# Queries written from PSUM into the heads' layout by two engines instead of six small DMAs, and a wait for output weights cut in two

## The reference, cut to what matters

```python
# layer 1, attention: latents = layernorm(x) [2, 512, 1024], H = 16 heads, KV = 4 groups of G = 4 heads, HD = 96
hidden = jnp.concatenate([context, latents], axis=1)            # 1536 rows
q = (latents @ Wq.T).reshape(b, q_len, H, HD)
k = (hidden @ Wk.T).reshape(b, s_len, KV, HD)
v = (hidden @ Wv.T).reshape(b, s_len, KV, HD)
scores = jnp.einsum('bkgqd,bksd->bkgqs', q, k) * scale
attn = jax.nn.softmax(scores, axis=-1)
out = jnp.einsum('bkgqs,bksd->bkgqd', attn, v)
return out.reshape(b, q_len, H * HD) @ Wo.T                     # added to x, times tanh(g_xattn[1])
# layer 1, feed-forward: router softmax, top 8 of 64 experts, mix of expert biases, added to x
```

## Time and profile before

| | us |
|---|---|
| median of 3 runs | 1075.05 (1074.87 to 1076.71) |
| profiled execution, its own time | 1076.0 |
| its span, first to last instruction | 1074.2 |
| PE busy | 1039.8 (97%) |
| DVE, ACT, POOL busy | 621.9, 620.1, 644.2 |
| units 0 to 127 start | 336.92 to 1026.02 |

### The profile page before, as it was taken

One profiled execution on the slowest core, in us unless ns is written; L12 is line 12 of the kernel. 1 busy time (PEld: TensorE's weight loads), 2 busy tenths in 40 slices (PEclk: granted clock), 3 DMA queues, 4 the chain that ended last, 5 costly groups with the idle time before them and its releaser, 6 DMA issues.

```text
span 1074.2 us, 18361 instructions
## 1 busy us (share of the span) xinstructions
PE 1039.8 (97%) x7242; PEld 587.5 (55%) x7242; DVE 621.9 (58%) x1068; ACT 620.1 (58%) x687; POOL 644.2 (60%) x348
## 2 busy tenths in 40 slices
PE   9999999999999989999999999999999999998895
PEld 4555434444544556566666666665665665555552
DVE  6889759654123555545545645655654655666666
ACT  5786435431223587665666765666765566577853
POOL 4476887242001588656668856658866667678751
PEclk9999999999999999999999999999999999999996
DMA  9886753842234999999999999999999999999993
GB/s 345 262 291 216 226 192 101 179 74 56 72 110 114 178 218 213 214 210 182 202 183 216 184 212 199 168 216 191 188 209 209 181 186 187 169 176 177 177 198 118
DMA packets 520265, 198.75 MB, mean 185 GB/s; under 512 B 485668, under 2 KB 500900, under 8 KB 520180
## 3 DMA queue, kind: packets, MB, share of 16 engines
q1 hardware_dynamic: 520180, 197.58, 88.3%
HBM read 56.88 MB, written 13.63 MB: 66 GB/s over the span
## 4 chain that ended last, share of the span: by engine, by line
PE 78%; POOL 9%; DMA 4%; DVE 3%; issue 3%; ACT 2%; SPq 1%; POOLq 0%; DVEq 0%; ACTq 0%
PE ps L566 27%; PE ps L806 21%; PE ps L780 12%; PE ps L821 10%; PE ps L823 5%; POOL p L1718 2%; POOL region_c L1718 2%; POOL region_y L1718 2%; DMA ln_t<-stage 1%; PE ps L588 1%; POOL x_res L1718 1%; DVE p_max L1553 1%; DMA region_o<-region_y 1%; PE ps L707 1%; DMA stage<-ctx_t_in 1%
## 5 line engine op out<-in xcount | busy, mean ns | idle before, releaser
L1718 POOL TENSOR_TENSOR region_y<-p,region_b 128x1536 f16<-128x1536 f32 x128 | 396.8, 3100 | 278.9 <-ACT region_b L1256 251.8
L1246 ACT ACTIVATE p<-ps,p_max 128x1536 f32<-128x1536 f32 x128 | 197.1, 1540 | 205.9 <-DVE p_max L1553 205.9
L1553 DVE TENSOR_REDUCE p_max<-ps 128x1 f32<-128x1536 f32 x128 | 225.0, 1757 | 131.3 <-PE ps L806 131.3
L806 PE MATMUL ps<-region_q,region_c 96*128 96x512 f16 x1152 | 269.9, 379 | 0.8 <-DMA region_c<-region_q 0.8
L821 PE MATMUL ps<-region_q,region_c 128*128 128x192 f16 x1536 | 207.6, 246 | 5.0 <-DVE logit L1578 3.4
L1256 ACT ACTIVATE region_b<-ps,p_max 128x1536 f16<-128x1536 f32 x128 | 196.4, 1534 | 25.9 <-DMA region_c<-region_b 25.6
L823 PE MATMUL ps<-region_q,region_o 128*128 128x96 f16 x1536 | 202.4, 206 | 0.0
L806 PEld LDWEIGHTS ps<-region_q,region_c 96*128 96x128 f16 x1152 | 105.3, 98 | 109.0 <-ACT region_b L1256 1.1
L821 PEld LDWEIGHTS ps<-region_q,region_c 128*128 128x128 f16 x1536 | 150.0, 98 | 21.7 <-DVE logit L1578 4.2
L823 PEld LDWEIGHTS ps<-region_q,region_o 128*128 128x128 f16 x1536 | 150.1, 98 | 13.9
L566 PE MATMUL ps<-region_w,region_q 128*128 128x512 f16 x576 | 136.1, 382 | 5.0 <-POOL region_w L1718 2.9
(11 more groups left out here) (149 smaller groups left out, 1105.7 us busy)
## 6 DMA issues: line engine op xcount, KB each, us to landing
stage<-ctx_in SPq DMA_DIRECT2D x16, 512.0 KB, 4.6
stage<-ctx_t_in SPq DMA_DIRECT2D x15, 512.0 KB, 8.7
stage<-wq_in SPq DMA_DIRECT2D x16, 384.0 KB, 4.0
stage<-wo_in SPq DMA_DIRECT2D x16, 384.0 KB, 4.3
k_scratch<-region_o SPq DMA_DIRECT2D x12, 384.0 KB, 6.5
region_q<-k_scratch SPq DMA_DIRECT2D x8, 576.0 KB, 5.6
region_q<-v_scratch SPq DMA_DIRECT2D x8, 576.0 KB, 6.1
x_res<-x_in SPq DMA_DIRECT2D x8, 512.0 KB, 8.7
```

The source lines that it names most:

```text
L806: ins = nc.tensor.matmul(bank(NSB * (m % 2) + sb_), q_head[0:HD, b, h, hq, qt * P:(qt + 1) * P], k_head[0:HD, b, hk, sb_ * 512:(sb_ + 1) * ...
L1246: nc.scalar.activation(p32[:, m % 2, :], rows, ACT.Exp, bias=p_max[:, m % 4:m % 4 + 1], accum_out=den[:, m % 4:m % 4 + 1]).then_inc(e32_ok, 1)
L1553: nc.vector.reduce_max(p_max[:, m % 4:m % 4 + 1], rows, axis=AX, negate=True).then_inc(max_ok, 1)
L1718: return nc.gpsimd.tensor_tensor(out, a, b, op)
```

## The change

Three parts.

1. On the host the columns of the query weights are put in another order within each group: block j gets the 96 columns of head j, and behind them columns 32j to 32j + 31 of head 3. So rows 0 to 95 of a product's block are head j, and rows 96 to 127 a third of head 3.
2. `take_q` and `take_low_q` write two pieces each, 96 partitions and 32 partitions, into `q_head` itself. `load_q`, `q_blk` and the semaphores `q_ld` are gone. `q_hi` and `q_free` count to two for a block; PE waits for `q_free` (six for a step) ahead of a step's first scores. From the third step on, ACT waits until the scores that read the old queries are done.
3. `out_product` with even w waits for the first two pieces of the output weights, with odd w for all four.

```diff
+        def q_rows(j):
+            own, last = slice(0, HD), slice(j * 32, (j + 1) * 32)
+            return ((j, own, own), (G - 1, last, slice(HD, P)))
...
-            def load_q(t, j):
-                sp.wait_ge(q_free, NJ * t + j + 1)
-                row = j * P
-                while row < (j + 1) * P:
-                    h, d = row // HD, row % HD
-                    n = min(HD - d, (j + 1) * P - row)
-                    sp.dma_start(q_head[d:d + n, t % B, h, :, :], q_blk[row - j * P:row - j * P + n, j, :, :]
-                                 ).then_inc(q_ld[t % B], 16)
-                    row += n
...
-                if q_end(m) is not None:
-                    if t > 0 and q_end(m) == 0:
-                        sp.wait_ge(sc_ready, UPS * t)
-                    load_q(t + 1, q_end(m))
...
-                    pe.wait_ge(q_ld[b], 6 * use(t, B))
+                    pe.wait_ge(q_free, 2 * NJ * (t + 1))
...
-                    pe.wait_ge(w_split, wo_n(w // 16) + RING)
+                    pe.wait_ge(w_split, wo_n(w // 16) + RING // 2 * (w % 2 + 1))
...
-                if t > 0:
-                    act.wait_ge(q_ld[(t - 1) % B], 6 * use(t - 1, B))
-                nc.scalar.activation(q_blk[:, j, HI, :], bank(at), ACT.Copy, scale=SCALE).then_inc(q_hi, 1)
+                if t >= B:
+                    act.wait_ge(sc_ready, UPS * (t - 1))
+                for h, rows, part in q_rows(j):
+                    nc.scalar.activation(q_head[rows, t % B, h, HI, :], bank(at)[part, :], ACT.Copy, scale=SCALE
+                                         ).then_inc(q_hi, 1)
...
-                dve.wait_ge(q_hi, n + 1)
-                nc.vector.scalar_tensor_tensor(q_blk[:, j, LO, :], bank(at), SCALE, q_blk[:, j, HI, :],
-                                               ALU.mult, ALU.subtract).then_inc(q_free, 1)
+                for k, (h, rows, part) in enumerate(q_rows(j)):
+                    dve.wait_ge(q_hi, 2 * n + k + 1)
+                    nc.vector.scalar_tensor_tensor(q_head[rows, t % B, h, LO, :], bank(at)[part, :], SCALE,
+                                                   q_head[rows, t % B, h, HI, :], ALU.mult, ALU.subtract
+                                                   ).then_inc(q_free, 1)
...
     wq = L1_xattn_Wq.T.reshape(NC, P, KV, QG).transpose(2, 1, 0, 3).reshape(KV * P, NC, QG)
+    order = np.concatenate([np.r_[j * HD:(j + 1) * HD, (G - 1) * HD + j * 32:(G - 1) * HD + (j + 1) * 32]
+                            for j in range(NJ)])
+    wq = wq[:, :, order]
```

More of the change, by code:

```diff
@@ L108, in flamingo @@
         v_head = view(region_q, 4 * SL, 2 * NS * VW).rearrange("p (b s w) -> p b s w", b=2, s=NS)
-        q_blk = view(region_q, 10752, NJ * 2 * QL).rearrange("p (j h s) -> p j h s", j=NJ, h=2)
         o_t = view(region_q, 13824, 2 * 2 * QG).rearrange("p (r h j q) -> p r h j q", r=2, h=2, j=NJ)
@@ L210, in flamingo @@
         v_ld = [sem(f"v_ld{b}") for b in range(B)]
-        q_ld = [sem(f"q_ld{b}") for b in range(B)]
         q_ready, q_hi, q_free = sem("q_ready"), sem("q_hi"), sem("q_free")
@@ L491, in _ @@
                 ring(s, stage[:, s, 0:c1 - c0], eb_d[:, c0:c1], w_split, W_WQ0 + s + 1)
-            for j in range(NJ):
-                load_q(0, j)
             sp.wait_ge(v_lo_ok, 5 * 4 + 2)
@@ L830, in _ @@
                 if j == 2:
-                    pe.wait_ge(q_free, 1)
+                    pe.wait_ge(q_free, 2)
                 q_product(6 + j % 2, 0, j, None)
@@ L861, in side_free @@
                     pe.wait_ge(v_lo_ok, 5 * 4 + 2 + sum(v in V_AT for v in before))
-                pe.wait_ge(q_free, NJ + sum(q_end(v) is not None for v in before))
+                pe.wait_ge(q_free, 2 * (NJ + sum(q_end(v) is not None for v in before)))
                 if any(wo_at(v) is not None for v in before):
@@ L1537, in take_low_q @@
             def take_low_q(n, at):
-                j = n % NJ
-                dve.wait_ge(q_hi, n + 1)
-                nc.vector.scalar_tensor_tensor(q_blk[:, j, LO, :], bank(at), SCALE, q_blk[:, j, HI, :],
-                                               ALU.mult, ALU.subtract).then_inc(q_free, 1)
+                t, j = n // NJ, n % NJ
+                for k, (h, rows, part) in enumerate(q_rows(j)):
[3 more added lines that the diff above has]
+                                                   ).then_inc(q_free, 1)
             def add_out(at, w):
```

## The result

Measured: 1069.57 us median (1068.31 to 1070.53, 6 runs) against 1075.89 (1074.87 to 1078.73, 6 runs) of the kernel before beside it, ratio 0.9937 [0.9923, 0.9950]: 6.8 us faster (5.4 to 8.3) by the ratio, 6.3 by the two medians. The kernel before was run anew beside each group of experiments; its median was then 1076.5 to 1077.5, so the medians of different groups are not to be subtracted. The forecast was 1071.4, its range 1069.9 to 1074.3. Profiled execution after: 1068.31, span 1066.5.

What follows compares the result with a forecast made beforehand. PE was taken as the bound, full from 428 to 945 us, so gains lie only before: 0.76 + 0.9 + 2.85 = 4.5, less 0.9 given back, is 3.6; 1075.05 - 3.6 = 1071.4 us, range 1069.9 to 1074.3.

Steps and rivals of the forecast that it cites:

- Part 1a: Unit 0: PE no longer waits for the first queries' DMAs; all 0.76 us gained.
- Part 1b: Step 0: four DMAs fewer bring transposes 2.4 us earlier (0 to 2.74); 0.9 of waits at units 10 and 11 mostly go.
- Part 3: Unit 12: output product 0 starts without waiting for POOL's fourth weight piece; 2.85 us gained there, nothing elsewhere.
- Given back by unit 20: By unit 17, about 0.9 of the 4.5 us gained is lost again to transposes in the dense DMA stretch.
- The wait named for it: A new PE wait of up to 1 us for a low half's transpose, about units 16 to 18.
- Part 2: Doubled query evictions on ACT and DVE: cost 0 from step 1 on, 0 to 0.1 at units 5 and 8.
- d: Time added per query block on DVE by the second piece: 0.61 us by the rows.
- The mechanism that the forecast set aside: DVE pieces at another start partition start later: added time 0.77, PE waits 0.15 at units 5 and 8, gain 3.3.
- the slower rival: Steps 1 to 6: PE waits for DVE's second piece once added time exceeds 1.21; 5.4 us slower at 1.6, 1080.4; chance 0.07.
- all of it stays: Rival: transposes follow PE, nothing is given back, 4.5 us gained, 1070.6 us; chance 0.24.
- the transposes keep their times: Rival: DMA engines stay full from 371 to 428 us, only 1.1 gained, 1074.0 us; chance 0.21.
- its chain starts from the last step's units and none of its work is touched: it moves as a whole: From 945 us on: despite long waits, the end only shifts with the earlier gain, adding or losing nothing.

Runs made afterwards that it cites:

- the pair of 1.45 against 1.20: DVE's two query pieces in the changed kernel, against the changed kernel with both pieces written at one start partition (head 3's queries wrong); one run, 1069.7 us.
- unit 12's matmuls: The kernel before with ten unread 512-column matmuls ahead of unit 12's wait for its output weights, nothing else: 1073.78 us, ratio 0.9977 [0.9966, 0.9987].

## Why the prediction was right and wrong

- **Part 1a, 0.76: right in kind, 0.93 measured** (3.09 - 2.16). The 0.17 more is how the ends of matmuls are drawn: the value product is drawn 4.06 long, and unit 0 starts 3.90 behind its start.
- **Part 1b, transposes relieved by 2.4: right in kind, and larger.** With spare DMAs in their place the stretch loses 1.14 from unit 0 to 20 instead of gaining 2.48 (2.22 in the second execution): 3.4 to 3.6 apart. The waits of units 10 and 11 went.
- **Part 3, 2.85 at unit 12: right at its place** (3.01 from unit 12 to 13 in the trace). Alone it keeps 0.2 of it by the trace.
- **Given back by unit 20: 0.9 forecast, 1.0 measured** (6.56 to 5.57). The wait named for it is there, 0.35 in unit 18, and 0.75 in unit 16 in the second execution, which gives back 1.25; the rest is spread over units 14 to 20.
- **Part 2: hidden from step 1 on, as said** (gain constant within 0.05 from unit 21 to 114 in every kernel). **Mis-sized in step 0:** there it cost 0.28 at unit 7 and again at unit 10, where 0 to 0.1 each was taken, because d is 0.84 and not 0.61. The mechanism that the forecast set aside is the one that the rows show: a piece that starts at another partition is held. By that rule it had 0.77 and 0.15 each, still too little. The Trainium skill states the rule ("VectorE: DVE Perf Modes", section "Two Vector instructions with no wait between them"); the pair of 1.45 against 1.20 agrees with it. On the forecast it took too little weight. It also disposes of the slower rival: 0.84 is below 1.21.
- **Sum by unit 20: 3.6 forecast, 3.41 and 3.15 measured.** The terms of the first are 0.93, less 0.56 for DVE's pieces, 1.03 for units 10 and 11, 3.01, less 0.99: each step is there, but that the sum is so near is in part luck, since what part 2 cost was made up by small surpluses elsewhere. Of the rivals neither "all of it stays" nor "the transposes keep their times" came in.
- **The step that failed: "its chain starts from the last step's units and none of its work is touched: it moves as a whole."** It gained 3.02 at unit 114: 1.38 by a shorter wait, 1.1 of it since DVE's 24 more instructions had moved a fetch away from the router's transposes, and 1.67 by the clock that had fallen behind the longer wait. The forecast's own table showed the clock at 0.91 for that stretch, and it was read as a property of the end, not as a price of single waits in it. Most of it is indeed the end's: the changed kernel still has 0.93. From unit 115 to the end of the span some 0.9 of it is given back in this pair of profiles (8.59 to 7.7).
- **The second half of the same fault is at unit 12.** The wait was priced at its length, 2.85. In some executions of kernels with this wait it was also followed by a half-clock stretch, and part 3 takes that along. Neither profile of before itself has it; that its runs do is inferred from the 2.5 that unit 12's matmuls gave. In the profile read for the forecast the clock there was 1.00, so its rows could not give the size. Of the 6.8 by the ratio, 3.4 + 3.0 - 0.9 = 5.5 stand in the pair of profiles; the remaining 1.3 lies within the interval (5.4 to 8.3) and in the size of what unit 12's matmuls gave (2.5, 1.4 to 3.7). How it is split between the two I can't say.

Not settled: why the same wait is followed by a low clock in one execution and not in the next, in units 12, 114 and 116 alike; what filling unit 116's wait would give, which no run tried; and why the router's transposes are issued 0.3 earlier in some executions.

## What to carry to other kernels

Price a wait of a few microseconds of TensorE as its length plus, in a share of the executions, a stretch at half clock behind it, and look for that share in more than one profile. Where such a wait can't be removed, unread matmuls into a free bank ahead of it are cheap and worth trying. And when an edit changes how many instructions an engine issues, expect waits for DMAs far from the edit to move: compare where the instruction fetches fall before giving the credit to the edit.

## What of the hardware was not expected

- Unread matmuls made the kernel before 3.8 us faster, and 24 one-column instructions on each of ACT and DVE 3.6 us.
- A fetch of 0.01 MB beside the router's transposes goes with a landing of 5.2 to 5.5 us instead of 4.2 to 4.5.
- ScalarE pays for a changed start partition too, as far as one pair of kernels shows it: a pair of pieces takes 1.20 against 1.06, VectorE's 1.41 against 1.29.
- The clock came back within 3 to 7 us in units 12, 114 and 116, but behind the last unit it stayed at 0.5 for ten, though PE was busy 7.81 of 10.
